# Five pairs of x sums made in the setup of a GRU and FFN kernel, and the setup's loads of pieces issued by SyncE

## The reference

```
def cell(h, x):
    gi = x @ W_ih + b_ih                 # 64 x 1536, does not depend on h
    gh = h @ W_hh + b_hh
    r = sigmoid(i_r + h_r); z = sigmoid(i_z + h_z)
    n = tanh(i_n + r * h_n)
    h_new = (1.0 - z) * n + z * h
...
y = x + ffn(scan(cell, cond_2048, x))    # ffn: quantise, gate and up, silu(g) * u, quantise, down
```

## Time and profile before

| | us |
|---|---|
| median of three runs | 2879.51 |
| span of the profiled execution, first to last instruction | 2879.2 |
| TensorE busy with matmuls | 2562.9 (89%) |
| VectorE busy | 1685.2 (59%) |
| ScalarE busy | 1140.6 (40%) |
| GpSimd busy | 1262.3 (44%) |
| window of t = 2, TensorE | 1533.2 to 1616.2 |
| first instruction of the plain steps' block | 2189.5 |

### The profile page before, as it was taken

One profiled execution on the slowest core, in us unless ns is written; L12 is line 12 of the kernel. 1 busy time (PEld: TensorE's weight loads), 2 busy tenths in 40 slices (PEclk: granted clock), 3 DMA queues, 4 the chain that ended last, 5 costly groups with the idle time before them and its releaser, 6 DMA issues. The chain is left out here.

```text
span 2879.2 us, 154632 instructions
## 1 busy us (share of the span) xinstructions
PE 2562.9 (89%) x67605; PEld 1681.0 (58%) x67605; DVE 1685.2 (59%) x3398; ACT 1140.6 (40%) x2317; POOL 1262.3 (44%) x598
## 2 busy tenths in 40 slices
PE   2088999998889999999999999999996999999995
PEld 1066777776768888887675564655642444444442
DVE  8852222225632222225646778867592888888887
ACT  1321222225632222224702333323232777777773
POOL 0255666662046666664061363622700333333334
PEclk8599999999999999999999999999998999999998
DMA  6833222224422222226554253442432223232322
GB/s 193 239 85 77 74 73 71 73 71 112 131 63 71 74 73 70 73 71 167 152 135 127 92 151 118 115 156 85 129 143 93 74 84 95 84 95 84 95 63 53
DMA packets 234843, 293.74 MB, mean 102 GB/s; under 512 B 69581, under 2 KB 194023, under 8 KB 233895
## 3 DMA queue, kind: packets, MB, share of 16 engines
q1 hardware_dynamic: 212743, 240.84, 30.6%
q10 hardware_dynamic: 18304, 36.19, 3.6%
q0 software_dynamic: 3680, 15.21, 1.9%
HBM read 231.61 MB, written 60.45 MB: 101 GB/s over the span
## 5 line engine op out<-in xcount | busy, mean ns | idle before, releaser
L1145 PE MATMUL psum<-second_shared 64*32 64x384 f16 x32768 | 1026.0, 324 | 50.2 <-issue 31.3
L1153 PE MATMUL psum<-low_w,low_hot 64*32 64x384 f16 x16384 | 756.5, 324 | 2.0 <-issue 2.0
L1372 DVE TENSOR_SCALAR second_shared<-psum 32x384 f16<-32x384 f32 x496 | 272.3, 549 | 749.1 <-PE psum L1145 741.9
L953 POOL TENSOR_TENSOR low_hot<-first_shared,sum_mask 128x1024 f16<-128x1024 f16 x256 | 499.8, 1952 | 430.1 <-DVE first_shared L1359 183.8
L1145 PEld LDWEIGHTS psum<-second_shared 64*32 64x32 f16 x32768 | 561.5, 93 | 198.0 <-issue 89.8
L947 POOL TENSOR_TENSOR second_shared<-first_shared,whole_mask 128x2048 f16<-128x2048 f16 x128 | 462.5, 3614 | 460.1 <-PE psum L1145 348.2
L1044 ACT ACTIVATE second_shared<-psum 32x384 f16<-32x384 f32 x496 | 239.8, 483 | 801.9 <-PE psum L1145 795.9
L1233 PE MATMUL psum<-low_w,low_hot 64*64 64x384 f16 x12288 | 513.7, 326 | 19.9 <-issue 13.5
L1233 PEld LDWEIGHTS psum<-low_w,low_hot 64*64 64x64 f16 x12288 | 378.3, 108 | 150.4 <-issue 18.4
L310 PE MATMUL psum<-w_x,x_cols 128*64 128x512 f32 (+1 forms) x1856 | 312.0, 495 | 9.5 <-ACT x_cols L280 9.5
L1153 PEld LDWEIGHTS psum<-low_w,low_hot 64*32 64x32 f16 x16384 | 282.5, 93 | 56.8 <-issue 3.1
(11 more groups left out here) (286 smaller groups left out, 2746.6 us busy)
## 6 DMA issues: line engine op xcount, KB each, us to landing
low_w<-w_rows SPq DMA_DIRECT2D x384, 144.0 KB
low_w<-w_rows SPq DMA_DIRECT2D x256, 120.0 KB
second_shared<-w_rows SPq DMA_DIRECT2D x1024, 24.0 KB, 1.9
x_gates<-x_out ACTq DMA_DIRECT2D x58, 384.0 KB, 2.3
xg<-x_gates SPq DMA_DIRECT2D x58, 384.0 KB, 3.2
low_w<-w_rows SPq DMA_DIRECT2D x256, 72.0 KB
low_w<-w_rows SPq DMA_DIRECT2D x384, 48.0 KB
w_rows<-quantised SPq DMA_DIRECT2D x24, 384.0 KB, 4.9
```

The source lines that it names most:

```text
L953: nc.gpsimd.tensor_tensor(low_hot[:, buf].rearrange("p (s k) b -> p s k b", s=SUBS), low_a[:, slot, bass.ds(c, 1), :, :].rearrange("p a s ...
L1145: last = nc.tensor.matmul(run[m][u][j * Q:(j + 1) * Q, :], whole_hot[rows[u], m, sign, kk, j % 2 * Q:(j % 2 + 1) * Q], whole_w[rows[u], m, ...
L1153: nc.tensor.matmul(run[m][u][j * Q:(j + 1) * Q, :], low_hot[rows[u], m, kk, j % 2 * Q:(j % 2 + 1) * Q], low_w[rows[u], m, at:at + UC], sta ...
L1372: last = nc.vector.tensor_scalar(whole_w[u * B:u * B + Q, m, 0, bq, :], run[m][u][bq * Q:(bq + 1) * Q, :], 1.0 / HIGH_ONE, None, ALU.mult)
```

## The change

The five first pairs are made at the end of TensorE's part of the setup, with weights `raw` and other PSUM banks; ScalarE's part of them stands in its chunk loop. The windows have 6 pairs each. SyncE issues the 48 loads of pieces, between its writes of chunks 2 to 5. The first four loads of x rows move to the start of the setup.

```
+            EARLY_PAIRS = 5
+            EARLY_BANKS = x_banks(1, (3, 4), (5, 0))
 # sync, setup, behind the three writes of chunk n
+                            if n == 2:
+                                sp.wait_ge(pieces_out, 2 * PIECES_OUT)
+                                load_low(sp, 0, LOW_ROWS, ROWS_X0)
+                            elif n == 3:
+                                load_whole(sp, 0, 0, ROWS_X0)
+                            elif n == 4:
+                                load_low(sp, H0, LOW_ROWS, ROWS_H)
+                            elif n == 5:
+                                load_whole(sp, H0, 1, ROWS_H)
 # scalar, setup
+                        def early_pair(j):
+                            for step in (2 * j, 2 * j + 1):
+                                take_out(a, step, EARLY_BANKS)
+                                if step + 2 < 2 * EARLY_PAIRS:
+                                    place_bias(step + 2, EARLY_BANKS)
+                                if step == 2 * j and j + 1 < EARLY_PAIRS:
+                                    copy_rows(a, j + 1, EARLY_BANKS)
+                        for j in range(2):
+                            load_rows(a, j)
 # in its loop over n, behind W3 of chunk n and scale_rows(n + 2); the same loads of pieces are gone from here
+                            if n == 1:
+                                a.wait_ge(x_cleared, 1)
+                                for step in range(2):
+                                    place_bias(step, EARLY_BANKS)
+                                copy_rows(a, 0, EARLY_BANKS)
+                            elif n - 2 in range(EARLY_PAIRS):
+                                early_pair(n - 2)
+                            if n >= CHUNKS - 2:
 # tensor, setup, at its end
+                        pe.wait_ge(plain_ok, 2 * PLAIN)
+                        x_pairs(pe, range(EARLY_PAIRS), raw, EARLY_BANKS)
 # window_of(t)
-                    return range(X_PAIRS * w // WINDOWS, X_PAIRS * (w + 1) // WINDOWS)
+                    late = X_PAIRS - EARLY_PAIRS
+                    return range(EARLY_PAIRS + late * w // WINDOWS, EARLY_PAIRS + late * (w + 1) // WINDOWS)
 # scalar, exact steps
-                        for j in range(2):
-                            load_rows(a, j)
-                            a.wait_ge(x_cleared, t - FINE + 1)
+                            a.wait_ge(x_cleared, t - FINE + 2)
```

## The result

The changed kernel took 2850.81 us (median of four runs, 2848.59 to 2851.29) against 2879.05 us for four runs of the kernel before: a ratio of 0.9902, 95% interval 0.9888 to 0.9916. That is 28.2 us less. The forecast was 2842.4 us in a range of 2836 to 2850; the time lies 0.8 us above it. Span and span: 2879.2 to 2849.5, 29.7 us less, where 37.1 were forecast.

The account below looks back on a forecast made before the run. Windows were taken to hold up stages and block's end; the setup had free TensorE time but busy ScalarE and DMA. -42.4 + 1.3 - 0.7 + 3.7 + 1.0 = -37.1 us from span 2879.2, plus 0.3: 2842.4 us, range 2836 to 2850.

Parts of the forecast that it names:

- Windows: Windows of t = 2, 3, 4, 7 to 6 pairs: the state becomes last, gains of 8.0, 7.9 and 8.25, sum 24.2 us.
- The last window: Block's end, 8 to 6 pairs: the state's second store becomes last, gain 18.8 us, bounds 17.8 and 22.1.
- the 0.6 us for the clock: TensorE idle about 3 us before each turn, then picking at half clock: cost 0.2 us a stage, bounds 0 and 0.8.
- Early pairs: Five pairs in the setup: first step 7.8 us, then 11.05 a pair, end at 128.4, with ScalarE keeping up.
- The tail (part 4): Setup's end: W3 of chunk 7 waits behind ScalarE's last copy and the ones for `whole_a`; cost 3.7 us, bounds 0 and 9.
- Start (part 3): Setup's start: four loads of x rows, 0.52 MB, delay VectorE's chain of cuts by 1.3 us, bounds 0 and 2.
- What was given back at the next block's start: Next block's start, relieved of the four x-row loads: gain 0.7 us, between 0 and 1.3.
- part 5: Setup, 71 to 131 us: more DMA traffic costs 1.0 us, bounds 0 and 8; SyncE issuing the loads costs 0.
- the 1.0 us for the DMA engines: Setup: 15.5 us of added DMA against 10.2 free, up to 5.3 us of backlog; cost taken as 1.0, bounds 0 and 8.
- DMA full in the setup: Rival: backlog makes VectorE wait for old writes at chunks 5 to 7; setup ends 12 us later, 2849 us; chance 0.16.
- The 0.3 us from span to time: Whole kernel: the median of the runs lies 0.3 us above the profiled span, added to 2842.1.

Follow-up runs that it names:

- SyncE's loads alone: Kernel before, with only the setup's 48 loads of pieces issued by SyncE; no early pairs or early x rows: 2878.54 us, ratio 0.9997.
- traffic with the loads spread: Kernel after, with SyncE's 48 loads of pieces spread, three behind each of its writes from chunk 1 on: 2848.43 us, ratio 0.9890.
- order without most of the traffic: Kernel after, ten early x stores cut to 16 of 768 columns, ten full stores added later (wrong gates): 2848.69 us, ratio 0.9898.

## Why the prediction was wrong

**Windows: right.** Forecast 8.0, 7.9 and 8.25 us for the windows of t = 2 to 4, measured 7.95, 7.82 and 8.22; the state took over as the last to be ready, as rows 1 to 3 said. The last window: 18.8 forecast, 19.35 measured, because from the state's second store to the next block took 2.6 us, not 3.1. Without the 0.6 us for the clock 43.0 were forecast in all, and 43.3 measured. The price for the clock shows only at the turn: it now runs at the lower clock (granted 0.50, 0.66 us instead of 0.44), and the pick starts 5.04 us behind it instead of 4.83. From the turn to the next window the stages moved by +0.1, +0.5 and -0.9 us, which hides it. The three idle microseconds that were forecast ahead of each turn were 3.8 to 5.7.

**Early pairs: right.** A first step of 7.58 us (7.8), then 11.06 a pair, last sums at 131.23 (128.4 plus the later start). ScalarE kept up with them.

**The tail (part 4): hidden.** Its 3.7 us could not show in the kernel after, since VectorE's own delay was longer. Where that was taken away the order of ScalarE's loop cost about 2 us. The prediction had noted that waits of VectorE up to 3.7 us lie in the tail's shade, and so it should have taken the larger of two terms and not their sum. Here the larger was 12.8.

**Start (part 3): under-sized.** 1.3 us with an upper bound of 2; measured 3.1, and 2.3 to 3.2 in the kernels that load the rows there. The sum took the bytes at the rate of the stretch before. But the rate itself fell, from 345 to 321 GB/s between 4 and 24 us: 0.48 MB less moved, and with the 0.52 MB of the rows about 1.0 MB, which at 321 GB/s is 3.1 us (an estimate). Why the engines moved less while as busy stays open. What was given back at the next block's start was 0.9, forecast 0.7.

**The step that failed is part 5**, "SyncE's 16 `load_low` issues [...] Chunks 4 and 5 go the same way, with 11 us each. Cost 0", and with it the 1.0 us for the DMA engines. Each was sized alone. The issue time was taken from ScalarE's row of a setup without the x traffic, 0.73 us. With it SyncE's four groups took 11.2, 12.9, 14.8 and 12.3 us, where the kernel with SyncE's loads alone took 9.2, 8.9, 11.3 and 10.0. The three groups ahead of chunk 5's writes took 9.6 us more, the six writes between them 3.4 more. The queue has no pause in which to catch up, so chunk 5's writes left 13 us late beyond the start's 3.5. The slack was sized at chunk 3's writes, the first behind the loads; at chunk 5's, the last that mattered, the order itself had left 1.3 us in hand. The prediction said that VectorE would begin to wait "if issuing were blocked for 5 us more"; it was, and this was priced neither in the sum nor fully in the rival. "DMA full in the setup", at 0.16, was the nearest case: SyncE's writes came late and VectorE waited for them, though the engines stood at 0.91. It had the setup 12 us later and 2849; 16.0 and 2850.8 came out. Its upper end should have set the range.

Two smaller things move the total. The 0.3 us from span to time compared the span of one execution with the median of others; the profiled execution of the kernel after took 2851.29 us, 1.8 above its span. And what lies outside the windows and the setup came out 2.3 us shorter, where only the 0.7 given back was forecast; the 1.6 between is luck, of the size by which executions differ there. Without it the total would have been further off.

Three runs beside the kernel after show it as an interplay: order without traffic, 0.2 us of waits or less; traffic with the loads spread, 6.6; order without most of the traffic, 0.9; both, 13.4 (13.95 in its second execution). What is left of it (6.0 to 9.8 us of waits in every kernel with the stores and spread loads) was not removed; moving the loads sooner did not help, and splitting the stores over later stages in earnest was not tried.

By the Trainium skill (DMA: Bandwidth & Descriptors, "Issuing engines are not separate DMA queues") all issuers share the 16 engines and a second issuer saves only issue time. The runs agree: pairs with ScalarE's loads end the setup 14.7 us later than with SyncE's, and the DMA share is 0.81 with SyncE's loads alone, against 0.83 before (71 to 131 us). The section calls issue time usually small beside the transfer; here, with the engines at 0.91 and not full, it was the issuer's time that was short.

## What to carry to other kernels

When work moves under another stage, price its DMAs by what they do to every issuing queue there, not by their own bytes, and follow each queue to the last transfer that somebody waits for, not only the first: a queue that fits with 0.70 us an issue (11.27 us for 16) does not with 0.92 (14.76). Where two delays end in the same wait, take the larger, and let the range reach the case in which a queue's slack is used up. The gain side came out within 1 us, because for each wait that went the next one in line was read from the trace.

## What the runs showed of the hardware

An issue costs its queue more when the x stores' bytes are on the DMA engines: SyncE's 48 loads took 39.4 us without the pairs, 41.4 with stores of 16 columns and 51.2 with full ones, at shares of 0.81, 0.86 and 0.91 between 71 and 131 us. The share of the moment does not give the price of a group, though: eight loads took 8.9 us at 0.93 (85 to 94 us, SyncE's loads alone), and 12.3 at 0.75 (127 to 140 us, kernel after). One of ScalarE's loads of x rows mostly took 0.5 to 0.6 us in a window and up to 2.6 us in the setup. And 0.52 MB at the head of a full stretch delayed the chunk behind it by 3 us: the engines stayed as busy, but from 9 to 14 us they moved 201 GB/s and not 299.
